# Router weights as 16 stationary columns, three folds instead of five, and a replanned instruction order

## The reference

```python
# long convolution over the pairwise products of 8 channels within each of 16 heads
kv = einsum('bhil,bhjl->bijhl', ctx, ctx)
y  = causal_convolution(kv, ssm_kernel) + kv * D
y  = einsum('bijhl,bhil->bjhl', y, layernorm(x))        # sum over the 8 channels i
x  = x + tanh(g_xattn) * y
z  = layernorm(x)
probs = softmax(z @ router_w + router_b); top 2, renormalised -> gates
mix = sum over e of gates[e] * gelu(z @ expert_w[e] + expert_b[e])
out = x + tanh(g_ffn) * (mix @ out_w + out_b)
```

## Time and profile before

| | us |
|---|---|
| median of 3 runs | 115.87 |
| lowest, highest | 115.85, 116.67 |
| profiled execution, its own time | 115.83 |
| its span, first to last instruction | 114.0 |
| PE busy in the span | 103.2 |

### The profile page before, as it was taken

One profiled execution on the slowest core, in us unless ns is written; L12 is line 12 of the kernel. 1 busy time (PEld: TensorE's weight loads), 2 busy tenths in 40 slices (PEclk: granted clock), 3 DMA queues, 4 the chain that ended last, 5 costly groups with the idle time before them and its releaser, 6 DMA issues.

```text
span 114.0 us, 1919 instructions
## 1 busy us (share of the span) xinstructions
PE 103.2 (90%) x574; PEld 86.3 (76%) x574; DVE 90.2 (79%) x293; ACT 57.2 (50%) x145; POOL 63.0 (55%) x83
## 2 busy tenths in 40 slices
PE   4956999989999999996679999999999999999960
PEld 4945888868999887754568888886788888888940
DVE  0283899999999998999889969777588876866940
ACT  4074377064258718641469997465645424353300
POOL 3015799999999999999999899600000000000000
PEclk9999999999999999999999999999999999999997
DMA  2867999159872410030030000000000101111031
GB/s 79 294 165 196 297 370 324 50 180 244 227 231 87 155 35 3 0 92 0 0 95 6 0 0 0 0 0 0 0 6 0 46 11 35 46 49 46 0 98 46
DMA packets 10956, 10.02 MB, mean 88 GB/s; under 512 B 1306, under 2 KB 10946, under 8 KB 10946
## 3 DMA queue, kind: packets, MB, share of 16 engines
q1 hardware_dynamic: 9570, 8.85, 26.6%
q10 hardware_dynamic: 1376, 1.05, 2.9%
HBM read 8.82 MB, written 1.07 MB: 87 GB/s over the span
## 4 chain that ended last, share of the span: by engine, by line
PE 61%; POOL 17%; DVE 13%; ACT 4%; issue 3%; POOLq 0%; DVEq 0%
PE ring L835 11%; PE ring L837 11%; PE ring L836 11%; POOL kv_t L374 10%; PE ring L756 6%; DVE zq_t L397 4%; PE ring L757 3%; PE ring L706 3%; DVE ow_lo_t L1040 2%; POOL w_lo_t L389 2%; ACT q_t L560 2%; PE red L779 2%; POOL rstd L403 2%; PE zbank L877 2%; PE red L712 2%
## 5 line engine op out<-in xcount | busy, mean ns | idle before, releaser
L1116 DVE SCALAR_TENSOR_TENSOR mix_t<-ring,ctxT_t,mix_t 128x256 f32<-128x256 f32 x55 | 26.6, 484 | 7.8 <-ACT ring L603 6.1
L603 ACT ACTIVATE ring<-ring 128x512 f32<-128x512 f32 (+1 forms) x33 | 18.7, 568 | 20.7 <-PE ring L837 20.7
L374 POOL TENSOR_TENSOR kv_t<-ctxT_t 128x320 f32<-128x320 f32 x27 | 23.7, 908 | 8.2 <-ACT ctxT_t L515 6.5
L835 PE MATMUL ring<-w_hi_t,zT_hi_t 128*128 128x512 f32 (+1 forms) x66 | 26.1, 396 | 0.0
L837 PE MATMUL ring<-w_hi_t,zT_lo_t 128*128 128x512 f32 (+1 forms) x66 | 25.4, 385 | 0.0
L836 PE MATMUL ring<-w_lo_t,zT_hi_t 128*128 128x512 f32 (+1 forms) x66 | 25.4, 384 | 0.0
L756 PE MATMUL ring<-kv_t,toep_t 128*128 128x288 f32 x64 | 20.9, 409 | 0.2 <-DVE zq_t L1021 0.2
L757 PEld LDWEIGHTS ring<-kv_t,toep_t 128*128 128x128 f32 x64 | 12.2, 190 | 3.3
L837 PEld LDWEIGHTS ring<-w_hi_t,zT_lo_t 128*128 128x128 f32 x66 | 12.4, 188 | 2.5
L835 PEld LDWEIGHTS ring<-w_hi_t,zT_hi_t 128*128 128x128 f32 x66 | 12.5, 189 | 2.3
L836 PEld LDWEIGHTS ring<-w_lo_t,zT_hi_t 128*128 128x128 f32 x66 | 12.5, 189 | 2.1
(11 more groups left out here) (124 smaller groups left out, 170.8 us busy)
## 6 DMA issues: line engine op xcount, KB each, us to landing
ctx_t<-in_L_ffn_expert_w SPq DMA_DIRECT2D x8, 256.0 KB, 4.3
toep_t<-kpad_dram SPq DMA_DIRECT2D x3, 512.0 KB, 6.6
x_t<-in_x SPq DMA_DIRECT2D x8, 128.0 KB
out<-x_t SPq DMA_DIRECT2D x8, 128.0 KB
wlast_t<-in_L_ffn_expert_w SPq DMA_DIRECT2D x1, 768.0 KB, 7.1
ctx_t<-in_ctx ACTq DMA_DIRECT2D x2, 256.0 KB, 3.0
zq_t<-in_x ACTq DMA_DIRECT2D x2, 256.0 KB, 3.7
ctx_t<-in_ctx SPq DMA_DIRECT2D x2, 256.0 KB, 4.2
```

Of the source, the lines that this page charges most:

```text
L374: eng.tensor_tensor(dst, head.unsqueeze(1).to_broadcast([P, HB + 1, HD * CB]), windows(ctxT_t, g, h, HB + 1), ALU.mult).then_inc(done, 1)
L603: act.activation(y, y, ACT.Gelu_apprx_tanh).then_inc(gelu_ready, 1)
L835: pe.matmul(y, hi, whi, start=(c == 0), stop=False)
L1116: dve.scalar_tensor_tensor(out=acc, in0=ring[n % RING][:, L * e:L * (e + 1)], scalar=gate, in1=acc, op0=ALU.mult, op1=ALU.add).then_inc(mi ...
```

## The change

- The router weights' high and low parts lie side by side in `rw_pair`. One matmul with 16 stationary columns makes high x high and low x high at once, in two rows of eight; high x low stays a matmul of 8 columns: 4 matmuls a group. The transposing of the logits becomes a float32 matmul with a 16 x 8 matrix of two stacked identities (`twice`, made by one more POOL instruction at the start), which also adds the two rows of eight.
- Folds: group 0 none; group 1 three, two on DVE (slots 4 to 0, 7 to 3) and one on POOL (5 to 1).
- `projection_low` (DVE, the split of the output weights) and `projection_high` (ACT) move behind the first accumulations of experts.
- The order on PE, DVE, ACT and POOL is replanned. The products done by DVE are 0, 2, 8, 23; `weights_low` of experts 0, 2 and 6 is DVE's. SP's order is unchanged.

```diff
-BY_VECTOR = (0, 5, 15, 22, 27)
-
-RELATIVE_BY_DVE, LOW_BY_DVE = (), (5,)
-FOLDED_BY_DVE = ((2,), (2, 3))
-FOLDED_BY_POOL = ((), (0, 1))
+BY_VECTOR = (0, 2, 8, 23)
+
+RELATIVE_BY_DVE, LOW_BY_DVE = (), (0, 2, 6)
+FOLDED_BY_DVE = ((), (0, 3))
+FOLDED_BY_POOL = ((), (1,))
+FOLDS = ((4, 0), (5, 1), (6, 2), (7, 3), (2, 0), (3, 1), (1, 0))
...
         def fold(eng, g, i, done):
 
-
             eng.wait_ge(read_out, (g + 1) * H)
+            for j, (_, into) in enumerate(FOLDS[:i]):
+                if into in FOLDS[i] or FOLDS[j][0] in FOLDS[i]:
+                    folded(eng, g, j)
+            src, dst = FOLDS[i]
             terms = zq[:, g].rearrange("p i n a -> p i (n a)")
-            eng.tensor_tensor(terms[:, i], terms[:, i], terms[:, HB + i], ALU.add).then_inc(done, 1)
+            eng.tensor_tensor(terms[:, dst], terms[:, dst], terms[:, src], ALU.add).then_inc(done, 1)
 
...
+            pool.wait_ge(identity_ready, 1)
+            pool.tensor_tensor(twice[:, :], ident[0:2 * E, 0:E], ident[0:2 * E, E:2 * E], ALU.add).then_inc(twice_ready, 1)
...
             first_inverse_std()
-            for n in range(2, 5):
+            for n in range(3, 8):
                 products(pool, n, pool_products_ready)
-            for n in range(6, 15):
+            for n in range(9, 14):
                 products(pool, n, pool_products_ready)
             scales(1)
-            for n in range(16, 22):
+            for n in range(14, 19):
                 products(pool, n, pool_products_ready)
             ones()
+            products(pool, 19, pool_products_ready)
+            products(pool, 20, pool_products_ready)
+            for n in range(0, 3):
+                relative(pool, n, weights_relative)
+            products(pool, 21, pool_products_ready)
+            products(pool, 22, pool_products_ready)
+            weights_low(pool, 1, weights_low_ready)
+            for n in range(24, 28):
+                products(pool, n, pool_products_ready)
+            scales(2)
             router_relative_rows()
-            products(pool, 23, pool_products_ready)
-            relative(pool, 0, weights_relative)
-            relative(pool, 1, weights_relative)
-            weights_low(pool, 0, weights_low_ready)
-            weights_low(pool, 1, weights_low_ready)
-            for n in range(24, 27):
+            for n in range(28, 32):
                 products(pool, n, pool_products_ready)
-            products(pool, 28, pool_products_ready)
-            products(pool, 29, pool_products_ready)
-            scales(2)
-            products(pool, 30, pool_products_ready)
-            products(pool, 31, pool_products_ready)
-            relative(pool, 2, weights_relative)
+            add_bias(0)
             relative(pool, 3, weights_relative)
-            weights_low(pool, 2, weights_low_ready)
-            fold(pool, 1, 0, pool_folded)
+            add_bias(1)
+            add_bias(2)
+            weights_low(pool, 3, weights_low_ready)
             fold(pool, 1, 1, pool_folded)
-            weights_low(pool, 3, weights_low_ready)
+            add_bias(3)
+            relative(pool, 4, weights_relative)
+            relative(pool, 5, weights_relative)
+            weights_low(pool, 4, weights_low_ready)
+            relative(pool, 6, weights_relative)
+            weights_low(pool, 5, weights_low_ready)
+            relative(pool, 7, weights_relative)
+            scales(3)
+            weights_low(pool, 7, weights_low_ready)
             for n in range(4, 8):
-                relative(pool, n, weights_relative)
-            weights_low(pool, 4, weights_low_ready)
-            add_bias(0)
-            scales(3)
-            weights_low(pool, 6, weights_low_ready)
-            weights_low(pool, 7, weights_low_ready)
-            for n in range(1, 8):
                 add_bias(n)
...
             split_weights(1)
+            split_weights(2)
             for n in range(1, 4):
                 statistics(B + n)
             scale_bias()
-            projection_high()
             for n in range(0, 4):
                 normalise(n)
-            z_high(0)
-            z_high(1)
-            split_weights(2)
-            z_high(2)
-            z_high(3)
+            for n in range(0, 4):
+                z_high(n)
             split_weights(3)
             activate(0)
+            route(0)
             activate(1)
-            route(0)
             activate(2)
             route_gates(0)
             activate(3)
+            split_weights(4)
             statistics(B + 4)
-            split_weights(4)
+            projection_high()
+            split_weights(5)
             statistics(B + 5)
+            activate(4)
             statistics(B + 6)
-            activate(4)
-            split_weights(5)
+            split_weights(6)
...
                 own = slice(BG * g, BG * (g + 1))
+                both = [rw_pair[:, 2 * E * c:2 * E * (c + 1)] for c in range(C)]
+                pe.matmul(red[0][0:2 * E, :], both[0], zT_hi[:, own, 0, :], start=True, stop=False)
                 for c in range(C):
-                    for n, (w, z) in enumerate(((rw_hi, zT_hi), (rw_hi, zT_lo), (rw_lo, zT_hi))):
-                        last = pe.matmul(red[0][0:E, :], w[:, E * c:E * (c + 1)], z[:, own, c, :],
-                                         start=(c == 0 and n == 0), stop=(c == C - 1 and n == 2))
-                last.then_inc(logits_ready, 1)
+                    pe.matmul(red[0][0:E, :], both[c][:, 0:E], zT_lo[:, own, c, :], start=False, stop=False)
+                pe.matmul(red[0][0:2 * E, :], both[1], zT_hi[:, own, 1, :], start=False,
+                          stop=True).then_inc(logits_ready, 1)
 
             def route_rows(g):
 
+                pe.wait_ge(twice_ready, 1)
                 pe.wait_ge(logits_evacuated, g + 1)
                 for b in range(BG):
-                    last = pe.transpose(red[1][:, E * b:E * (b + 1)], lgT_sb[:, P * b:P * (b + 1)], ident[0:E, 0:E])
+                    last = pe.matmul(red[1][:, E * b:E * (b + 1)], lgT_sb[:, P * b:P * (b + 1)], twice[:, :],
+                                     start=True, stop=True)
                 last.then_inc(logit_rows_ready, 1)
...
+            for n in range(0, 14):
                 convolve(n)
             queries(2)
-            convolve(16)
-            convolve(17)
+            convolve(14)
             queries(3)
-            convolve(18)
+            for n in range(15, 19):
+                convolve(n)
+            sum_channels(0)
+            sum_channels(1)
             convolve(19)
+            sum_channels(2)
+            convolve(20)
+            sum_channels(3)
+            for n in range(21, 28):
+                convolve(n)
             for n in range(0, 3):
-                sum_channels(n)
-            convolve(20)
-            convolve(21)
-            sum_channels(3)
-            for n in range(22, 30):
+                z_transposed(n)
+            convolve(28)
+            z_transposed(3)
+            for n in range(29, 32):
                 convolve(n)
-            z_transposed(0)
-            z_transposed(1)
-            convolve(30)
-            z_transposed(2)
-            z_transposed(3)
-            convolve(31)
             experts(0, *BLOCKS[0])
+            route_logits(0)
             experts(1, *BLOCKS[1])
-            route_logits(0)
+            route_rows(0)
             experts(2, *BLOCKS[2])
-            route_rows(0)
             experts(3, *BLOCKS[3])
...
-            products(dve, 15, dve_products_ready)
-            for n in range(11, 16):
-                query_products(n)
-            fold(dve, 0, 2, dve_folded)
-            products(dve, 22, dve_products_ready)
-            query_products(16)
-            router_split()
+            products(dve, 23, dve_products_ready)
+            query_products(17)
             residual(0)
-            for n in range(17, 20):
-                query_products(n)
+            weights_low(dve, 0, dve_weights_low_ready)
+            query_products(18)
             residual(1)
+            query_products(19)
+            weights_low(dve, 2, dve_weights_low_ready)
             residual(2)
             query_products(20)
-            products(dve, 27, dve_products_ready)
-            query_products(21)
             residual(3)
-            for n in range(22, 30):
+            for n in range(21, 27):
                 query_products(n)
-            z_low(0)
-            z_low(1)
-            query_products(30)
-            query_products(31)
-            z_low(2)
+            router_split()
+            query_products(27)
+            for n in range(0, 3):
+                z_low(n)
+            query_products(28)
             z_low(3)
-            fold(dve, 1, 2, dve_folded)
+            for n in range(29, 32):
+                query_products(n)
+            fold(dve, 1, 0, dve_folded)
             fold(dve, 1, 3, dve_folded)
-            projection_low()
             choose_values(0)
```

(74 more changed lines are left out.)

24 lines of the change are left out of this document (13 added, 11 removed).

## The result

| | before | changed |
|---|---|---|
| median, us | 115.90 | 123.60 |
| lowest to highest | 115.85 to 116.67 | 121.07 to 126.48 (4 runs) |
| profiled execution, its span | 115.83, 114.0 | 121.07, 119.3 |
| ratio to the kernel before | | 1.047 (1.037 to 1.057) |

Forecast were 119.3 and at most 121.0: the direction held, and the forecast loss was too small. Of the 4.3 us between 119.3 and the median of 123.6, the profile of the shortest execution accounts for 1.8 (121.07 against 119.3); the other 2.5 come from the longer executions, of which there is no profile.

The account below looks back on a forecast made before the run. PE was taken as the bound, busy 103.2 of 114.0 us. POOL's wait and the folds delay `experts(4)` by 3.4 us, plus 0.1 after it: span 117.5, median 119.3 us, range 117.6 to 121.0.

Parts of the forecast that it names:

- The moved `relative(2)`: On POOL, now ahead of products 21 and 22: reached by about 31.9, it waits 4 to 5 us for `bias_in[2]`.
- The arrival T: When bias 2 lands for POOL's `relative(2)`: issue at 33.54 on SP plus 2.5 us, T = 36.0.
- rival B: Bias 2 queues behind weights 3, T = 37 to 37.9: +4.5 to +5.4, 120.4 to 121.3 us; chance 0.15.
- What follows T: POOL's queue after the bias: product 31 at T + 13.4, its fold at T + 18.15; `experts(4)` at 62.5.
- the mark: Start of `experts(4)` on PE, saturated from there: forecast at 62.5 against 59.07, +3.4 us.
- The folds: Group 1's folds on DVE and POOL exclude each other, ending at 58.6, when the first sum starts.
- Behind the mark: PE after `experts(4)` starts: sum 7 adds 0.23, group 1 logits save 0.46, rows add 0.34: +0.1 us.
- A: DVE and POOL folds exclude each other little, PE's own work bounds: +2.2 + 0.1, 118.2 us; chance 0.15.
- C: `relative(2)` on POOL does not wait: `experts(4)` at 56.9, in all -2.0, 113.9 us; chance 0.13.
- D: Nothing to measure: POOL's wait smaller or refunded by removed PE idling, T near 33, 115.9 us; chance 0.07.

Follow-up runs that it names:

- the bias first: Changed kernel with two SP DMA issues exchanged, bias 2 ahead of weights 3: 120.35 us, ratio 1.035 (1.022 to 1.047).
- the kernels without the wait: Changed kernel with expert 2's trio (`relative(2)`, weight split, `weights_low(2)`) moved back: 115.83 us; changed kernel with SP fetching three experts early (`EARLY = 3`): 115.21 us.
- the gap filled: Changed kernel with 22 idle transposes on PE before `convolve(21)`: 120.46 us, ratio 1.033 (1.022 to 1.044); measured again, 121.14 us beside the changed kernel's 121.48.

## Why the prediction was right and wrong, point by point

- **The moved `relative(2)`: right.** POOL was there at 31.3 (between 30.7 and 31.9), stood for the bias, and the convolutions, DVE's `weights_low` and all behind them came late. Taking the wait away brings `experts(4)` 5.8 us forward, and putting it alone into the old kernel costs 4.5 us of the time.
- **The arrival T: the step that failed.** I took T = 36.0 from an issue at 33.54 and 2.5 us of landing; it was 37.44, from 34.01 and 3.43. Of the 1.44 us, 0.47 is the issue, which moves from execution to execution (33.2 to 35.3 in all profiles with weights 3 ahead of it), and 0.9 the landing, which moves too (1.5 to 3.7). In five of the six profiles of the table above T was 36.75 to 38.43, later than I took it, and in one 35.75. So T was a spread that lay mostly above my value, and I read the issue from one execution only. The value was that of rival B; whether its reason, queueing behind weights 3, is the cause stays open.
- **What follows T: right.** Forecast were 26.5 us from T to `experts(4)`. Measured: 63.84 - 37.44 = 26.40; 61.77 - 35.34 = 26.43 with the bias first; 26.43, 26.38 and 26.39 in the three further profiles. The slope of one holds over 3 us of T (35.34 to 38.43). With the measured T the prediction's own sum gives 62.5 + 1.44 = 63.9 for the mark, and 63.84 was measured.
- **The folds: right in size.** 59.6 against 58.6 + 1.44 = 60.0 for their end, with DVE's last. The rule of exclusion held, but not that the lock changes hands at the next instruction (below).
- **Behind the mark: a term too small.** +0.1 was forecast, it was +0.53. The rows cost 0.99, above the upper bound of 0.68: I had priced a float32 record at that of a transpose by dividing 0.34 by four, but eight records cost 0.124 each. That is 0.31 of the missing 0.43; the other 0.12 I can't place.
- **Total.** 1.44 (T) - 0.1 (the path from T) + 0.43 (behind the mark) = 1.8 us, from 117.5 to the 119.3 of the measured span. The upper end of the range, 121.0, was called B's middle; the middle of B's own 120.4 to 121.3 is 120.9.
- **The spread: not foreseen.** The kernel before varies by about 1% in most executions (four of its 51 took 117.3 to 121.1 us) and the changed one by 5%; this is what lifts the median from 121 to 123.6, and its cause is open. That the clock would fall was not in the prediction either. In the two profiles of the changed kernel it cost nothing by `experts(4)`; in the old kernel with the call moved it cost some 1.3 us by `experts(0)`.
- **Rivals.** A (folds side by side) was wrong: DVE's two folds took 5.36 us beside POOL's. C and D needed a bias that comes early; C's account is what the kernels without the wait show, 1.3 to 1.9 us off, since it had PE's work too small and left out that the chain of folds and gates ends only just in time.

## What to carry to other kernels

Before an instruction is moved forward in an in-order queue, read for each of its waits when the thing waited for arrives, also where the old trace shows no wait, because there it was hidden: here one line of SP's queue, the issue at 33.54 of a bias wanted at 31 or 32, told that POOL would stand. The better cure here was at the other end: with the DMA ahead instead of the instruction back, the same order went from 4 to 5% slower to 1% faster. And fewer matmuls were no gain here, since the step after them turned from four transposes into eight float32 records.

## What was not expected of the hardware

- A 1 KB transfer took 1.5 to 3.7 us from issue to use behind a 256 KB one in SP's order (six profiles), and 2.0 us ahead of it (one). The spread is larger than the difference that the order could be seen to make.
- A DVE fold can stand through many of POOL's instructions: 5.5 us for a fold of 1.2 us, through six instructions without a pause. In other places of these traces it got its turn at the next boundary (the first fold of the changed kernel, 54.27, was done 1.1 us after POOL's instruction ended at 55.2). The Trainium skill ("SBUF — State Buffer", its two separate sides) says that the loser blocks for the whole instruction; the trace agrees, and adds that it can be longer than one. What decides who gets it was not tried.
- After waits of PE of 2.5, 3.8 and 4.1 us (changed kernel twice, old kernel with the call moved) the granted clock fell to 0.50 (1.2 GHz) for 3.4 to 6.8 us. It stayed at 1.00 through the 1.46 us wait of the kernel before and through one of 1.76 us in the kernel without POOL's fold. With the gap filled it stayed up.
